# A graph-attention layer on one Trainium2 core: a reordered ScalarE step, a GpSimd subtraction held behind the attention planes, value products in one batch

## The reference, cut to what matters

```python
q = x @ wq.T + bq                      # x is 384 x 1024, weights 1024 x 1024
k = x @ wk.T + bk
v = x @ wv.T + bv
q2 = (q @ wiq.T + biq).reshape(N, H, D).transpose(1, 0, 2)     # N=384, H=16, D=64
k2 = (k @ wik.T + bik).reshape(N, H, D).transpose(1, 0, 2)
v2 = (v @ wiv.T + biv).reshape(N, H, D).transpose(1, 0, 2)
mask = _build_mask(edge_index, edge_type, edge_type_weights, x.dtype)
scores = einsum('hnd,hmd->hnm', q2, k2) / sqrt(D) + mask[None]
attn = softmax(scores, axis=-1)
out = einsum('hnm,hmd->hnd', attn, v2).transpose(1, 0, 2).reshape(N, 1024)
x = layernorm(x + out @ wo.T + bo)
```

## Time and profile before

| | us |
|---|---|
| median of 3 runs | 302.81 |
| lowest and highest | 300.88, 303.5 |
| the profiled execution's own time | 302.12 |
| its span (first to last instruction) | 300.2 |

### The profile page before, as it was taken

One profiled execution on the slowest core, in us unless ns is written; L12 is line 12 of the kernel. 1 busy time (PEld: TensorE's weight loads), 2 busy tenths in 40 slices (PEclk: granted clock), 3 DMA queues, 4 the chain that ended last, 5 costly groups with the idle time before them and its releaser, 6 DMA issues.

```text
span 300.2 us, 5086 instructions
## 1 busy us (share of the span) xinstructions
PE 285.0 (95%) x1578; PEld 248.3 (83%) x1578; DVE 189.6 (63%) x434; ACT 161.8 (54%) x304; POOL 144.6 (48%) x130
## 2 busy tenths in 40 slices
PE   8999999999999999999987999999999998999990
PEld 8999999999999988889986596868676776676880
DVE  5799966775667763225284858686868686821085
ACT  5953443234432344321485978878787878763023
POOL 2000665535365545519876346465656565577000
PEclk9999999999999999999997999999999999999997
DMA  7969864444643369562149285756566666660013
GB/s 276 330 243 323 234 204 150 151 150 140 226 173 104 131 216 354 200 209 81 70 149 207 84 157 164 136 169 128 172 125 174 123 177 120 161 139 0 2 70 140
DMA packets 51918, 49.27 MB, mean 164 GB/s; under 512 B 41056, under 2 KB 41920, under 8 KB 51776
## 3 DMA queue, kind: packets, MB, share of 16 engines
q1 hardware_dynamic: 49792, 47.63, 53.9%
q0 software_dynamic: 1680, 0.62, 1.0%
q10 hardware_dynamic: 432, 0.85, 0.8%
HBM read 37.44 MB, written 2.21 MB: 132 GB/s over the span
## 4 chain that ended last, share of the span: by engine, by line
PE 70%; DVE 14%; ACT 7%; issue 7%; DVEq 1%; ACTq 1%
PE bank L911 19%; PE bank L902 13%; PE bank L903 13%; PE bank L904 13%; PE bank L985 5%; PE bank L1004 4%; ACT scratch L536 3%; PE bank L927 3%; DVE row_inv L808 3%; DVE shared L820 2%; ACT shared L524 2%; DVE shared L800 2%; ACT h_hi L501 2%; DVE h_lo L775 2%; DVE stats L876 1%
## 5 line engine op out<-in xcount | busy, mean ns | idle before, releaser
L390 POOL DMA_INDIRECT mask_cells<-scratch x48 | 52.6, 1097 | 72.6 <-DMA mask_cells<-scratch 30.3
L441 ACT ACTIVATE w_hi<-w_raw 128x1024 fp32r<-128x1024 f32 x49 | 51.5, 1052 | 21.1 <-PE bank L911 21.1
L902 PE MATMUL bank<-x_hi,w_hi 128*128 128x384 f32 x176 | 58.8, 334 | 0.0
L903 PE MATMUL bank<-x_lo,w_hi 128*128 128x384 f32 x176 | 58.8, 334 | 0.0
L904 PE MATMUL bank<-x_hi,w_lo 128*128 128x384 f32 x176 | 58.8, 334 | 0.0
L902 PE MATMUL bank<-h_hi,w_hi 128*128 128x384 f32 x128 | 47.1, 368 | 3.0 <-DVE h_lo L775 3.0
L353 POOL TENSOR_TENSOR w_lo<-w_raw,w_hi 128x1024 fp32r<-128x1024 f32 x18 | 42.7, 2393 | 12.6 <-ACT w_hi L441 12.6
L631 DVE TENSOR_TENSOR w_lo<-w_raw,w_hi 128x1024 fp32r<-128x1024 f32 x31 | 37.8, 1223 | 16.2 <-ACT w_hi L441 15.2
L484 ACT ACTIVATE h_hi<-bank,bcol 128x384 f32 (+1 forms) x24 | 13.9, 580 | 56.4 <-PE bank L904 56.4
L904 PE MATMUL bank<-h_hi,w_lo 128*128 128x384 f32 x128 | 43.5, 340 | 0.0
L903 PE MATMUL bank<-h_lo,w_hi 128*128 128x384 f32 x128 | 43.4, 339 | 0.0
(11 more groups left out here) (100 smaller groups left out, 475.8 us busy)
## 6 DMA issues: line engine op xcount, KB each, us to landing
w_raw<-weights SPq DMA_DIRECT2D x53, 512.0 KB, 3.3
shared<-key_rows SPq DMA_DIRECT2D x6, 512.0 KB, 4.1
shared<-start SPq DMA_DIRECT2D x5, 320.0 KB, 6.0
res<-x_rows SPq DMA_DIRECT2D x1, 1536.0 KB, 6.6
out<-res SPq DMA_DIRECT2D x6, 256.0 KB, 2.0
mask_cells<-scratch POOLq DMA_INDIRECT x48
shared<-start ACTq DMA_DIRECT2D x2, 320.0 KB, 5.1
mask_cells<-mask SPq DMA_DIRECT2D x1, 576.0 KB, 6.2
```

Source lines behind the costliest of these rows:

```text
L390: nc.gpsimd.indirect_dma_start(out=mask_cells, out_offset=bass.IndirectOffsetOnAxis(ap=cell[:, c:c + 1], axis=0), in_=cell_value[:, c:c + ...
L441: nc.scalar.activation(w_part(t, s, slice(0, F))[0], w_raw[:, s, :], ACT.Copy).then_inc(w_hi_done, 1)
L902: pe.matmul(out_ps, w_hi[:, s, cols], moving_hi, start=(k == 0), stop=False)
L903: pe.matmul(out_ps, w_hi[:, s, cols], moving_lo, start=False, stop=False)
```

## The change

Five things are moved, nothing is computed differently:

1. POOL's second low part of a step moves behind `v_low`, and it first waits until all six low planes of the step's attention are done (`plane_lo_done`, 6j). In the last step the same is done for tile WO_TILE+3.
2. ACT makes the k tile's high part ahead of `att_high`, no longer behind it.
3. PE's 18 value products stand in one batch behind the q tile's eighth block, no longer six each behind blocks 5, 6 and 7.
4. In step 1 alone, ACT and DVE take the q tile's high and low part inside the attention (after the first four exponentials; after the sixth masking), no longer behind it.
5. SP's order of issues is not touched.

```diff
--- before.py
+++ after.py
@@ POOL: step @@
-                low_part(t + LEAD + 1, s0 + 1)
                 if not (isinstance(j, int) and j < 1):
                     v_low(j - 1, 1 - par)
+
+                    pool.wait_ge(plane_lo_done, 2 * NT * j)
+                low_part(t + LEAD + 1, s0 + 1)
@@ POOL: after the loop @@
             low_part(WO_TILE + 2, 2)
+            v_low(PAIRS - 1, 1)
+            pool.wait_ge(plane_lo_done, 2 * NT * PAIRS)
             low_part(WO_TILE + 3, 3)
-            v_low(PAIRS - 1, 1)
@@ ACT: softmax @@
-            def softmax(a):
+            def softmax(a, q_tile=None):
                 exps(a, range(0, 4))
+                if q_tile is not None:
+                    evacuate(*q_tile)
                 high_planes(a, (0,))
@@ ACT: step @@
-                if attend:
+                q_tile = (t, L1_TILES + 2 * j, par, 0)
+                if not attend:
+                    evacuate(*q_tile)
+                elif not more:
+
+                    softmax(a, q_tile)
+                else:
                     softmax(a)
-                evacuate(t, L1_TILES + 2 * j, par, 0)
-                if more:
+                    evacuate(*q_tile)
                     for h in range(2):
                         att_half_out(j - 2, h)
+                evacuate(t + 1, L1_TILES + 1 + 2 * j, par, 1)
+                if more:
                     att_high(j - 2)
-                evacuate(t + 1, L1_TILES + 1 + 2 * j, par, 1)
@@ DVE: attention, step @@
                 mask_scores(a, 5)
+                if q_tile is not None:
+                    evacuate_pair(*q_tile)
                 low_planes(a, (0, 1))
@@ PE: step @@
-                        if which == 0 and more and k >= VALUES_FROM:
-                            values(j - 2, par, k - VALUES_FROM)
+                    if which == 0 and more:
+                        for m in range(NT):
+                            values(j - 2, par, m)
```

More of the change, by code:

```diff
@@ L47 @@
 SCORE_PLACE = 3
-VALUES_FROM = 5
 LEAD = 2
@@ L822, in low_planes, with attention @@
                                                    op0=ALU.mult, op1=ALU.subtract).then_inc(plane_lo_done, 1)
-            def attention(a):
+            def attention(a, q_tile=None):
                 if isinstance(a, int) and a == 0:
@@ L841, in step @@
                 more = not (isinstance(j, int) and j < 2)
+                q_tile = (L1_TILES + 2 * j, par, 0)
                 if isinstance(j, int) and j < 1:
-                    evacuate_pair(L1_TILES + 2 * j, par, 0)
+                    evacuate_pair(*q_tile)
+                elif not more:
+                    attention(a, q_tile)
                 else:
                     attention(a)
-                    evacuate_pair(L1_TILES + 2 * j, par, 0)
-                if more:
+                    evacuate_pair(*q_tile)
                     for h in range(2):
```

## The result

| | before | after |
|---|---|---|
| median of 4 runs, us | 303.15 | 332.42 |
| lowest and highest, us | 300.88, 303.95 | 331.51, 333.21 |
| profiled execution, own time and span, us | 302.12, 300.2 | 332.98, 330.9 |

The change makes the kernel slower by 9.8%: ratio 1.098, 95% interval 1.091 to 1.105. That is 29 us, and the work is the same (the counts of instructions of PE, DVE, ACT and POOL are equal).

The account below looks back on a forecast made before the run. PE, busy 95% of the span, was taken as the bound; the added wait makes a ring. 169.5 + 7 x 17.9 = 294.8, plus 0.1, 30.55 and 0.7, span 326.15; plus 1.92 outside: 328.1 us, range 320 to 335.

Parts of the forecast that it names:

- The ring: POOL's wait, SP's load, four transposes and DVE's masking form a loop between attentions: step 17.9 us, before 14.9.
- the transposes aren't held: Rival on SP: the transposes go out without waiting for the low part, so only gains count: 293 us; chance 0.05.
- hand-overs: Four hand-overs between engines in each round, estimated at 0.1 us each: 0.4 us.
- the load ahead of the transposes: On SP's queue: transposes right behind a 512 KB load lose nothing to about 1 us; taken as 0.5 us.
- L(0): Landing of attention 0's last transpose, from which seven rounds follow: 169.5 us (169.0 to 170.2).
- slow clock: PE behind a wait: 1.5 us, fitting into each step's slack; ahead of the last values 0 to 1.5, taken 0.7.
- the rival with PE at the lower clock for a whole step: Each PE wait leaves the clock low all step, 14 us becoming some 20: 337 us and above; chance 0.07.
- PE's waits: PE waits about 3.8 us ahead of the values in each step, for a transpose; none before the scores.
- The parts that remove waits: ACT's order, early q tile, POOL away from DVE, batch of values: about 9 us less if nothing else moved.
- ScalarE's order alone: ACT's k tile ahead of `att_high` frees the chain before the scores: at most 3.4 us, some 5 with weight loads.
- The early q tile: Step 1's q tile inside the attention: PE's 3.04 us wait and 1.5 us slow stretch go, 4.5 us at most.
- POOL off DVE: DVE's chain loses 1.27 us per step at L808, about half a microsecond at L820; worth something only where late.

Follow-up runs that it names:

- Experiment 1: The kernel before with only POOL's part of the change (second low part behind `v_low` and its wait for the low planes): 332.67 us.
- experiment 3: The changed kernel with SP issuing an attention's four transposes ahead of the weight load that waits for POOL's second low part; POOL's wait kept: 294.24 us.
- experiment 4: The changed kernel without POOL's wait for the low planes; the second low part stays behind `v_low`: 300.90 us.
- 5: The changed kernel with half 1's low plane in memory of its own, so DVE's fourth masking waits for no transpose: 324.83 us.
- experiment 2: The changed kernel with POOL's order put back as before, all other parts of the change kept: 297.09 us.
- 8: The kernel before with POOL's part of the change and SP's four transposes ahead of the weight load: 296.58 us.
- experiment 6: The changed kernel with SP's weight load issued behind the four transposes, SP still waiting for POOL's second low part ahead of them: 322.62 us.

## Why the prediction came out as it did

**The mechanism was right.** The ring was predicted from POOL's wait over SP's queue to DVE's masking, with all its links: POOL waits for L830, SP for L352, DVE for the DMA, PE for the DMA and no longer for DVE. Experiment 1 shows that it needs no other part of the change, 3 that it passes through SP's order, 4 that it needs the wait, 5 that DVE's masking closes it. The rival "the transposes aren't held" gave 293 us for the case that SP's order lets them out; that case is experiment 3, 294.24 us.

**The time was 332.4 us, 4.4 above the forecast of 328 and inside 320 to 335.** Its terms against the measured ones, for the round from 190.00 to 208.52:

| term | predicted us | measured us |
|---|---|---|
| fourth masking to last low plane | 6.82 | 196.20 + 0.63 - 190.00 = 6.83 |
| POOL's low part | 2.37 | 2.41 |
| SP's load issue | 0.33 | 0.33 |
| first to last transpose's issue | 4.21 + 0.5 | 5.13 |
| landing of the last transpose | 3.3 | 3.25 |
| hand-overs (the rest) | 0.4 | 0.57 |
| sum | 17.93 | 18.52 |

So the term that was mis-sized is the one without a row, the load ahead of the transposes: bounded by 0 and 1 us, taken as 0.5 us, it measured 5.13 - 4.21 = 0.92 us in this round and 0.71 us on average of the seven, all of it at the issues and nothing at the landing. The hand-overs are the other one, 0.17 us more than estimated (the landing is handed to DVE's masking in 0.26 us, not 0.1). Seven rounds of 18.39 us, (300.32 - 171.60) / 7, in place of 17.9 make 3.4 us.

The Trainium skill (DMA: Bandwidth & Descriptors, "Queues, rings and completion order") says that on each DMA engine the descriptors of one queue are consumed in ring order. The prediction read 18.4 us for a step out of it. The measured step agrees in size, but in part by luck, since the load's share is 0.71 us and not the 1 us of that reading; the order of the descriptors themselves is shown by no run.

The second part is L(0), 171.60 us against 169.5. Of its 2.1 us, 1.3 lie ahead of the attentions (the first masking starts at 150.93 where it started at 149.59, on work that the change doesn't touch; in the other versions it starts between 149.48 and 151.55), and 0.6 us are the landing in the first round, which took 3.87 us. Against these, no slow clock followed PE's last wait (it was 1.19 us, not 3), which gives 0.7 us back. Together 3.4 + 2.1 - 0.7 = 4.8 us, and the profiled execution took 332.98 us against the 328.1 of the sum.

Two numbers around the forecast were worked out wrongly, without harm to it. The upper end of L(0) is 159.2 + 2.4 + 0.5 + 4.2 + 3.3 + 1.0 = 170.6 us, not 170.2, so all high ends give 333.5 us, still inside the range. And the rival with PE at the lower clock for a whole step put its 14 us at some 20, where the prediction's own row (half the speed) gives 28; it did not happen: the mean granted clock of the changed kernel is 0.955.

**PE's waits** were predicted at 3.8 us in each step; they are 28.2 us in eight, 3.5 on average. Their spread, 1.2 to 7.0 us, comes in part from the clock. In the windows behind two of them (columns as in the earlier trace rows) the granted clock was 0.50 behind the wait of 7.01 us, so the lower level, 1.2 GHz, and 1.00 behind a wait of 2.75 us, and the values took 5.21 and 3.76 us:

```profile
171.60:174.60 3.00, 3.00 (x9) 0.82 (x10) 2.39 (x9) 2.15 (x6) 0.00 (x0) 0.50 0.13 51
...
189.90:192.90 3.00, 3.00 (x16) 1.10 (x16) 2.39 (x9) 2.20 (x7) 0.00 (x0) 1.00 0.39 143
```

A slow stretch eats into the wait that comes next: the two waits that follow values at full clock are 4.47 and 4.20 us, the five that follow slow values (0.50 to 0.60) are 1.19 to 3.86 us. The rest of the spread is not explained. As predicted, the slow clock fits into the slack: the four steps that begin with values at 0.50 to 0.52 are 18.27 to 18.35 us, no longer than the mean.

**The parts that remove waits** were put at about 9 us together. Version 3, in which they all work, gains 302.91 - 294.24 = 8.7 us. That this agrees, and with it the 293 us of the rival, is in part luck: the two terms that make up the 9 us are worth 5.8 us (experiment 2), and 2.9 us come from POOL's part, to which the sum gave nothing. One by one they were less well sized. ScalarE's order alone was put at 3.4 to 5 us at most and gives 2 us: the term ignored that DVE's chain stays held, and that the q tile's low part is the next thing to be late. The early q tile was put at up to 4.5 us and gives 3.0. POOL off DVE was called worth something only where the chain is late; it is 2.9 us between versions 2 and 3, and 6 us on the kernel before, with SP's move (8).

## What to carry to other kernels

A wait that is added on one engine is paid on every queue that waits for that engine, so follow the semaphore into the DMA queues in the order of issue, and ask what stands behind the instruction that waits. When the late transfer feeds the very work that the new wait waits for, the cost is not a delay but a ring, and its length, added up from rows, is the new step. The cure was to reorder the queue, not to drop the wait: the same edit on POOL costs 30 us behind one order of issues and gains 6 us behind another.

## What the runs showed of the hardware

- DMA transposes issued right behind a weight load of 512 KB on the same queue: in the seven rounds of the changed kernel one issue of four takes 1.84 to 2.37 us in place of 1.3 to 1.4, and the list of DMAs gives a median landing of 3.9 us for the high planes' transposes (3.3 us with the load behind them, experiment 6). From the first issue to the last landing the four take 8.2 us on average, against 7.5 us in experiment 6. Why the issues are slower is not shown.
- A DVE operation that reads two SBUF tensors was held until about the end of a POOL subtraction that ran on two SBUF tensors, however small it was: 1.70 us for 128 x 3 elements that take 0.15 us. In experiment 4 two low planes took 3.64 us in place of 1.68. The masking, which reads one operand from PSUM, was not: 0.56 us with POOL busy beside it and without.
